# Feed-forward front of a macaron block: logits one group behind the transposes, two buffers of normalised rows, the first mask product behind one routed tile

## The reference

```python
x = x + 0.5 * ffn(layernorm(x))
x = x + attention(layernorm(x))
x = x + 0.5 * ffn(layernorm(x))

def ffn(x):
    scores = sigmoid(x @ gate_w.T + lb_bias)           # 8 experts
    topw, topi = top_k(scores, 2)
    topw = topw / (topw.sum(-1) + 1e-08)
    for e in range(8):
        m = topi == e
        wmean = (topw * m).sum() / max(m.sum(), 1)     # one number per expert, over all rows
        out += where(m.any(-1), mlp_e(x) * wmean, 0)
    return out + mlp_shared(x)                         # mlp: silu(x @ gw.T) * (x @ uw.T) @ dw.T
```

## Time and profile before

| | |
|---|---|
| median of 3 runs | 794.42 us (792.17 to 795.18) |
| profiled execution | 796.0 us, span 794.2 us |
| TensorE busy | 740.2 us, 93% of the span |
| VectorE busy | 579.5 us, 73% |
| ScalarE busy | 420.5 us, 53% |
| GpSimd busy | 42.2 us, 5% |
| mean granted TensorE clock | 0.946 of 2.4 GHz |
| chain that ended last | TensorE 50%, VectorE 14%, no visible wait 11% |

### The profile page before, as it was taken

The page is one execution under the profiler, slowest core; times in us unless marked ns, Lnnn a source line. Parts: engine busy times, 40 slices in busy tenths (PEclk is TensorE's granted clock), DMA queues, the critical chain, the costliest instruction groups (busy, mean ns, idle before and its releaser), DMA issues.

```text
span 794.2 us, 15242 instructions
## 1 busy us (share of the span) xinstructions
PE 740.2 (93%) x5580; PEld 345.4 (43%) x5588; DVE 579.5 (73%) x1937; ACT 420.5 (53%) x610; POOL 42.2 (5%) x60
## 2 busy tenths in 40 slices
PE   5889998987899999999999999999999778899998
PEld 3633444544244444444444444444433466344443
DVE  5776333757989999999999999999995276643311
ACT  2423342422077777767777767767777633333211
POOL 3200001110000000000000000000000022000000
PEclk9799999985579999999999999999999988999999
DMA  7001000354100100011001101011000000000012
GB/s 203 1 0 16 0 1 0 118 171 127 50 12 26 36 28 26 19 37 36 19 20 35 36 20 28 26 35 37 19 19 2 2 1 1 0 1 0 1 40 66
DMA packets 37983, 26.15 MB, mean 33 GB/s; under 512 B 12026, under 2 KB 37242, under 8 KB 37908
## 3 DMA queue, kind: packets, MB, share of 16 engines
q1 hardware_dynamic: 37332, 25.09, 11.2%
q10 hardware_dynamic: 576, 0.08, 0.1%
HBM read 14.64 MB, written 10.26 MB: 31 GB/s over the span
## 4 chain that ended last, share of the span: by engine, by line
PE 50%; DVE 14%; issue 11%; ACT 2%; another core or an unknown queue 0%; DVEq 0%; ACTq 0%
PE ps L958 46%; DVE mx L848 7%; PE ps L963 4%; DVE mx L841 1%; ACT h_all L569 1%; DVE xn L648 1%; DVE h_all L841 1%; DVE h_all L659 1%; DVE stats L636 1%; DVE wb L869 0%; DVE mm_ L866 0%; PE ps L1006 0%; DVE mv L640 0%; ACT xnT_all L490 0%
## 5 line engine op out<-in xcount | busy, mean ns | idle before, releaser
L569 ACT ACTIVATE h_all<-ps 128x1024 f32<-128x1024 f32 (+3 forms) x384 | 291.5, 811 | 120.4 <-PE ps L958 117.2
L848 DVE TENSOR_REDUCE mx<-ps 128x1 f32<-128x512 f32 (+2 forms) x352 | 222.8, 681 | 9.1 <-PE ps L958 6.1
L958 PE MATMUL ps<-ks,xnT_all 57*128 57x512 bf16 (+3 forms) x768 | 183.4, 342 | 12.5 <-DVE mx L841 7.3
L958 PE MATMUL ps<-h_all,vb 128*32 128x512 f32 (+3 forms) x1536 | 163.9, 500 | 0.6 <-ACT osb L558 0.6
L958 PE MATMUL ps<-xnT_all,ks 59*128 59x512 bf16 (+3 forms) x768 | 159.4, 333 | 3.3 <-ACT h_all L569 3.2
L841 DVE CUSTOM_DVE_ANT_0 h_all<-ps,mask_w 128x384 bf16<-128x384 f32 (+1 forms) x256 | 149.2, 618 | 3.7 <-issue 2.0
L958 PEld LDWEIGHTS ps<-ks,xnT_all 57*128 57x128 bf16 x768 | 57.6, 95 | 144.9 <-DVE mx L841 68.7
L659 DVE TENSOR_TENSOR h_all<-ps,sg 128x512 f32<-128x512 f32 x80 | 55.0, 690 | 81.8 <-PE ps L958 50.5
L958 PE MATMUL ps<-cb 64*128 64x64 bf16 (+3 forms) x1216 | 113.6, 217 | 0.0
L486 ACT ACTIVATE sg<-ps 128x512 f32<-128x512 f32 x80 | 47.6, 597 | 101.1 <-PE ps L958 80.0
L958 PE MATMUL ps<-xnT_all,wg 128*128 128x512 f32 x160 | 88.6, 637 | 1.0 <-ACT sg L486 0.9
(11 more groups left out here) (119 smaller groups left out, 529.6 us busy)
## 6 DMA issues: line engine op xcount, KB each, us to landing
xnT_all<-q_scr SPq DMA_DIRECT2D x64, 96.0 KB
q_scr<-qp SPq DMA_DIRECT2D x8, 384.0 KB
ks<-k_scr SPq DMA_DIRECT2D x64, 48.0 KB
x<-in_x SPq DMA_DIRECT2D x8, 256.0 KB, 6.9
q_scr<-qp SPq DMA_DIRECT2D x8, 256.0 KB
out<-x SPq DMA_DIRECT2D x8, 256.0 KB, 2.3
k_scr<-kp SPq DMA_DIRECT2D x48, 32.0 KB
xnT_all<-bias_scr SPq DMA_DIRECT2D x64, 18.0 KB
```

The lines of the kernel that those rows point to most:

```text
L569: act.activation(pr[:, (NSTEP * i + s) % PR_BUFS, p:HPG:SLOTS, lo:HALF], ps[:, b:b + 2, lo:HALF], ACT.Exp)\
L848: dve.tensor_reduce(m, src, AX.X, V.max).then_inc(a_out, 1)
L958: return pe.matmul(o, l, r, start=start, stop=stop, skip_group_check=True)
```

## The change

Three things. In the front, TensorE does the logits of group c - 1 behind the transposes of group c and ahead of the shared pair, instead of the logits of group c behind the pair; the last group's logits follow the first of the late shared pairs. `xn` has two buffers, and `ln_apply(c)` waits for `turn(c - 2)` only. In the first group's routed tiles one pair stands ahead of the first mask product, instead of two.

```diff
-        xn = sb("xn", [P, GT, P])
+        xn = sb("xn", [P, 2, GT, P])
...
             def ln_apply(c, par, s_rs, s_T, s_xn):
-                after(dve, s_T, c)
+                after(dve, s_T, c - 1)
                 dve.wait_ge(s_rs, c + 1)
                 for t in range(GT):
-                    ins = dve.tensor_scalar(xn[:, t, :], x[:, c * GT + t, :], mv[:, par, t, 0:1],
+                    ins = dve.tensor_scalar(xn[:, par, t, :], x[:, c * GT + t, :], mv[:, par, t, 0:1],
                                             rstd[:, par, t:t + 1], V.subtract, V.mult)
...
-                def front(c, par, first, last):
-                    pe.wait_ge(f.xn, c + 1)
-                    after(pe, f.xA, c - 1)
-                    turn(lambda t: xn[:, t, :], 7 * par).then_inc(f.T, 1)
-                    if c == 1:
-                        pe.wait_ge(s_w, 16 * len(ffn_loads))
-                    if 0 < c <= LATE_SHARED:
-                        up(c - 1, 1 - par, MT, xnT_all[:, c - 1, :], None)
+                def logits(c, par):
                     pe.wait_ge(f.xA, c + 1)
                     after(pe, f.lg, c - 1)
                     for t in range(GT):
                         ins = mm(ps[:, 1 + par, EXPERTS * t:EXPERTS * t + EXPERTS], xnT_all[:, c, t * P:(t + 1) * P],
                                  gate_w[:, :])
                     ins.then_inc(f.gl, 1)
+
+                def front(c, par, first, last):
+                    pe.wait_ge(f.xn, c + 1)
+                    after(pe, f.xA, c - 1)
+                    turn(lambda t: xn[:, par, t, :], 7 * par).then_inc(f.T, 1)
+                    if not first:
+                        logits(c - 1, 1 - par)
+                    if c == 1:
+                        pe.wait_ge(s_w, 16 * len(ffn_loads))
+                    if 0 < c <= LATE_SHARED:
+                        up(c - 1, 1 - par, MT, xnT_all[:, c - 1, :], None)
...
                 def routed_tiles(c, par, first, last):
 
-                    late = 2 if first else 1
                     if first:
                         mask_T(0, 0)
-                    for n in range(late):
-                        gate_and_up(GROUPS + MT * c + n, n % 2, n, xnT_all[:, c, :])
+                    gate_and_up(GROUPS + MT * c, 0, 0, xnT_all[:, c, :])
                     pe.wait_ge(f.mk, c + 1)
-                    for n in range(late):
-                        mask_gate(n % 2, n, maskT[:, par, :])
-                    for n in range(late, MT):
+                    mask_gate(0, 0, maskT[:, par, :])
+                    for n in range(1, MT):
                         up(GROUPS + MT * c + n, n % 2, n, xnT_all[:, c, :], maskT[:, par, :])
-                        if n == late and not last:
+                        if n == 1 and not last:
                             mask_T(c + 1, 1 - par)
...
                 for c in range(LATE_SHARED, GROUPS):
                     up(c, c % 2, MT, xnT_all[:, c, :], None)
+                    if c == LATE_SHARED:
+                        logits(GROUPS - 1, 1)
...
-                    turn(lambda t: xn[:, t, :], 4).then_inc(f.Tb, 1)
+                    turn(lambda t: xn[:, c % 2, t, :], 4).then_inc(f.Tb, 1)
```

## The result

Measured: 799.53 us (median of 8 runs, 796.32 to 802.13) against 794.80 (8 runs, 792.17 to 797.09). The ratio is 1.0059, 95% interval 1.0037 to 1.0081: the change makes the kernel 2.9 to 6.4 us slower, 4.7 by the middle. The forecast was 796.3, in a range of 790 to 801.5, with a small loss as the likeliest case.

What follows compares the result with a forecast made beforehand. VectorE was taken to pace the fronts' middle, 3.14 us a group, with a slow clock at their ends. Starts 1.6 and 1.3, ends +2.9, choice -1.7, mask -1.7 per FFN gave +1.9 on 794.42: 796.3 us, range 790 to 801.5.

Steps and rivals of the forecast that it cites:

- Edit 1a: Fronts' starts: logits(0) now ahead of the shared pair delays VectorE, 1.6 and 1.3 us, together 2.9, bounds 1.3 to 4.5.
- the late case: First front's start: clock rises one stage later, next groups' transposes and logits run slow, product of group 1 2.4 us late.
- Edit 1b: Fronts' ends: last logits stand behind group 4's shared pair, clock falls again, 2.9 us more at each end.
- a clock that is back early: Front's end: clock returns for the pair's second half, 8.8 us from turn(6) to the last add, 2.0 more.
- a slow end: Front's end: all at 1.2 GHz, 10.5 us from turn(6) to the last add, 3.8 more than before.
- What arrives: Choice of experts, last add to mask copy: 1.7 us of waits for groups 4 and 5 take up delay first.
- Edit 2: First routed tiles: one pair instead of two ahead of the first mask product, a gain of 1.7 us per FFN.
- Edit 3: Second xn buffer: brings nothing in the first FFN's down stage; its effect in the fronts is counted there.
- The sum: Both FFNs: +1.1 us in the first and +0.8 in the second, +1.9 together, 796.3 us.
- Rival A: Ends of both fronts: clock stays at 2.4 GHz, -5.5 us, 789; one front -2 to -3; chances 0.13 both, 0.07 one.
- Rival B: Choice of experts: clock falls a second time while TensorE waits, 1.9 us more per FFN, 802 with slow ends; chance 0.23.
- Rival C: Whole kernel: no edit's effect arrives, VectorE's pace and the choice set all, within 1 us of 794.4; 0.57 with the forecast.

Runs made afterwards that it cites:

- experiment 1: Changed kernel with the old first routed tiles, two pairs ahead of the mask product: 803.72 us, ratio 1.0101 to the kernel before.
- experiment 3: Changed kernel with the last group's logits ahead of the shared pair of group 4: 793.69 us, ratio 0.9996 to the kernel before.
- experiment 8: Changed kernel with three unused products of 384 columns in its 1.91 us wait ahead of turn(6), group 6's transposes: 792.35 us, ratio 0.9955 to the kernel before.
- experiment 2: Kernel before with only the mask edit, the first mask product behind one routed tile: 790.99 us, ratio 0.9939 to the kernel before.
- experiment 4: Changed kernel with the logits of group 0 directly behind their own transposes, as before: 794.79 us, ratio 0.9992 to the kernel before.
- experiment 5: Changed kernel with both front ends repaired: group 0's logits behind their transposes, last logits ahead of group 4's shared pair: 793.00 us, ratio 0.9963 to before.
- experiment 6: Mask edit on the old front, plus five unused products of 384 columns in the waits of groups 5 to 7: 787.15 us, ratio 0.9899 to before.
- experiment 11: Mask edit on the old front's order, plus two xn buffers: 792.69 us, ratio 0.9963 to the kernel before.
- experiment 10: Changed kernel with unused products ahead of both fronts and between the transposes of groups 0 and 1: 789.44 us, ratio 0.9933 to the kernel before.
- experiment 12: Changed kernel with unused products ahead of both fronts, between the transposes of groups 0 and 1, and at the front's end: 784.85 us, ratio 0.9871 to before.
- experiment 9: Mask edit on the old front with unused products in all front waits, start, end and ahead: 781.01 us, ratio 0.9825 to the kernel before.
- experiment 7: Mask edit on the old front, unused products at the front ends and ahead of both fronts: 785.70 us, ratio 0.9878 to the kernel before.

## Why the forecast held, point by point

- **Edit 1a, the start.** Right in kind, too small. Forecast 1.6 and 1.3 us. The changed kernel and experiments 1, 3 and 8, with the new start and no filling ahead of it, have a mean start of 23.3 us; those with the old start order and none (before, 2, 4, 5, 6, 11) 21.3. That is 1.9 us an FFN, 3.9 together instead of 2.9, and the repair measured 5.3. The step that was mis-sized is "I take the middle, 1.6", and still more the 1.3 of the second FFN: the 0.41 us wait that went there freed nothing, since the product of group 0 was waited for anyway. The middle was too low because its upper bound was summed wrongly. The recorded terms, 18.1 + 0.9 + 1.7 + 1.7 + 0.9, end at 23.3 us, and the product of group 1 had started at

```profile
19.80 0.68 DVE L659 TENSOR_TENSOR h_all<-ps,sg 128x512 f32<-128x512 f32 x1
```

so the late case is 3.5 us or more late, not 2.4. The second front of experiment 1 shows it: its start is 25.04 us, 4.1 above before. That the slow clock makes the loss is shown by experiments 10 and 12: with it gone, the same order has starts of 19.4 to 20.7 us, no longer than the old order's in experiment 9 (21.07 / 19.43).
- **Edit 1b, the end.** Right. Forecast 2.9 us more at each front's end; the changed kernel and experiments 1 and 4 have a mean of 13.1 against 10.1 us of before, 2 and 11: 2.9 to 3.0 (2.7 with experiment 10, which has the same end). The two cases that were weighed both occur: the changed kernel's second front took 8.70 us from turn(6) to the last add, forecast 8.8 for a clock that is back early, and the first fronts of experiments 1 and 4 took 10.40, forecast 10.5 for a slow end. That the middle fits is part luck, as it depends on how often each happens. So are the 9.46 us of the changed kernel's first front, within the 8.8 to 10.5: turn(6) and logits(5) still ran fast there, where the sum has them slow, and turn(7) then waited 1.18 us for the apply, where the sum has no wait. The cause of the loss is the last logits behind the shared pair, at the slow clock: experiment 3 takes the place back (5.0 us in the ratio) and experiment 8 holds the clock up, in its trace in one of the two fronts, and gives 8.3. Against the changed kernel's own trace, its fastest run, the stages of the two FFNs are shorter by 2.7 us in experiment 3 and by 5.5 in experiment 8, less than the ratios say.
- **What arrives.** Right. Forecast 1.7 of each delay absorbed in the choice; 9.13 fell to 7.36, and taken from the mean of before, 2 and 11 (8.9) it is 1.5.
- **Edit 2.** Right. Forecast -1.7 in each FFN, measured -1.72 in the stage, and 3.3 (experiment 1 against the change) and 4.8 us (experiment 2) in the time.
- **Edit 3.** Forecast nothing by itself; none is to be seen (experiment 11). Its cost is new: it lets the apply of group 7 start just as the memset begins, 2.41 us instead of 1.87. At the slow clock this is hidden behind logits(6) in the old order; in the new one turn(7) waited 1.18 us for it, where I had it hidden. Rival A's price for it, 1.4 us where the clock is fast, is seen in experiment 8: with the clock still at 1.00, turn(7) waited 1.05 us for that apply in the first front.
- **The sum.** With the measured stages, 2 x (1.9 + 2.95 - 1.5 - 1.7) = 3.3 us, within the measured 2.9 to 6.4; the forecast had 1.9 and the medians show 4.7. The forecast's sign and range were right and its size too small. The start's term accounts for 1.0 of the missing 2.8 us and the choice's for 0.4; the other 1.4 are not attributed.
- **Rival A**, the clock stays up, did not happen by itself. It was brought about by experiment 8, in the second front of its trace: 0.9955, 3.6 us below the kernel before, where A in one front had -2 to -3 and A in both 789 (0.993).
- **Rival B**, a second fall during the choice, was not seen: the changed kernel's trace has 1.00 in its waits of 0.82, 0.43 and 0.67 us, and the routed tiles start fast in all traces. It stays possible in runs without a trace.
- **Rival C**, nothing arrives, is refuted by the four single edits, each of which moved the time.

The Trainium skill ("TensorE: Matmul & The Clock Gate", HAM oscillation) was cited against the change, for its gathered idle time. The traces agree in kind: the bursts behind the one wait are slow. But that wait is 1.91 us, shorter than those of the page's own example, and the old order's three waits of 0.6 to 0.7 us did the same; filling either (experiments 6 and 8) is what helped. Of the skill's exclusive lock ("SBUF — State Buffer", Who interferes with whom): the trace agrees, the apply that began 0.05 us behind the memset ended 0.66 us behind the memset's end, 1.3 us longer than the usual 1.12.

Why does experiment 6 show only about half of its stages' gain in the whole? In the traces, its two FFNs are 6.6 us shorter than those of experiment 2, but "between" is 5.4 longer (594.6 and 589.2 in the table). The granted clock of two stretches of it, the down half with the start of the attention, and the attention's end; experiment 2 and then experiment 6:

```profile
120.00:240.00 120.00, 105.40 (x601) 50.03 (x603) 91.53 (x335) 43.52 (x74) 9.68 (x11) 0.82 0.28 81
...
600.00:640.00 40.00, 30.91 (x329) 18.10 (x321) 13.83 (x44) 23.38 (x35) 0.55 (x1) 1.00 0.01 2
```

```profile
120.00:240.00 120.00, 107.21 (x603) 50.56 (x603) 91.95 (x335) 44.36 (x74) 9.68 (x11) 0.77 0.28 83
...
600.00:640.00 40.00, 32.83 (x317) 19.70 (x315) 11.25 (x30) 22.48 (x34) 0.00 (x0) 0.91 0.01 2
```

From 240 to 600 us the clock is 1.00 in both. So where no edit touches the program, the clock was low for 17 us more in the trace of experiment 6. Over the 14 traces "between" goes from 589.2 us (44 us at the low clock) over 591.9 to 592.2 (51 to 55) and 592.5 to 593.8 (58) to 594.3 to 595.0 (61). What stays open is why it differs from run to run and whether an edit in the front moves it, and so how much of the ratios of single experiments, 3, 4 and 8 above all, is the edit's own.

## What to carry to other kernels

Moving a small step "one behind" to hide its wait pays only if the wait was on the path; look at the two ends of the loop, where there is no neighbour to hide it and where what was moved lands ahead of something that everybody waits for. Here the middle of the loop gained nothing, and each end lost 2 to 3 us. Where TensorE has short waits in front of a dense stretch, look at the granted clock before reordering: a few unused products in the waits gave 0.4% at one place and, at all places together, turned the old front from 0.994 into 0.983. Where the clock changes from run to run, cut the span into stages and compare those; here 5 us came and went where no edit was. A change of several edits should be timed edit by edit: this one held a gain of 0.6% (the mask) under a loss of 1%.

## What the runs showed of the hardware

Five unused products of 384 columns at each front's end, in waits of 0.6 to 0.7 us, kept the granted clock at 1.00 through both fronts' ends, where it had been 0.50 for 10 us. In the first front of experiment 7, filling that ended 0.5 us before the work began was of no use, as the clock fell among the next short waits, of 0.69 and 0.33 us. An apply of 1.12 us took 1.87 when it began 0.58 us behind a memset on GpSimd, and 2.41 when it began 0.05 us behind it. The column of the granted clock can read 1.00 at the start of a program where the lengths show the low level. And identical kernels differ by 5 us from run to run here (792.17 to 797.09 for the kernel before), with the mean granted clock of the changed kernel's runs going from 0.950 in the fastest to 0.938 in the slowest, 802.13.
